# The lower steps of a tree of column maxima as one strided reduction, in a graph attention kernel

## What is computed

```
h = x @ W
e = leaky_relu((h @ a_src)[src] + (h @ a_dst)[dst], 0.2)
m = segment_max(e, dst)
ex = exp(e - m[dst])
out = segment_sum(ex * h[src], dst) / (segment_sum(ex, dst) + 1e-16) + b
```

## Time and profile before

| What | Value |
|---|---|
| Median of 3 runs | 9346.27 us (9345.22 to 9348.08) |
| The profiled execution | 9340.91 us |
| Its span, first to last instruction | 9339.1 us |
| Instructions | 124921 |
| VectorE busy | 7033.1 us (75%) |
| GpSimd busy | 6762.4 us (72%) |
| TensorE busy | 4710.7 us (50%) |
| ScalarE busy | 4614.9 us (49%) |

### The profile page before, as it was taken

One profiled execution on the slowest core, in us unless ns is written; L12 is line 12 of the kernel. 1 busy time (PEld: TensorE's weight loads), 2 busy tenths in 40 slices (PEclk: granted clock), 3 DMA queues, 4 the chain that ended last, 5 costly groups with the idle time before them and its releaser, 6 DMA issues. The chain is left out here.

```text
span 9339.1 us, 124921 instructions
## 1 busy us (share of the span) xinstructions
PE 4710.7 (50%) x23458; PEld 4311.8 (46%) x23458; DVE 7033.1 (75%) x11854; ACT 4614.9 (49%) x12210; POOL 6762.4 (72%) x6887
## 2 busy tenths in 40 slices
PE   5777777777344444444444444444443444444444
PEld 4666666666344444444443444444443333333333
DVE  6888888888557777777777777777776777777777
ACT  4777777777334444444443444444443444444443
POOL 4777777777237777777767777777776777777776
PEclk8666666666655555555555555555555555555555
DMA  2222222222111111111111111111111111111111
GB/s 70 55 55 55 57 55 55 55 55 55 54 44 31 31 31 31 31 31 31 31 27 30 31 31 31 31 31 31 31 31 28 33 32 32 33 32 32 33 33 29
DMA packets 674668, 358.57 MB, mean 38 GB/s; under 512 B 548403, under 2 KB 549299, under 8 KB 674243
## 3 DMA queue, kind: packets, MB, share of 16 engines
q0 software_dynamic: 219264, 236.37, 13.5%
q1 hardware_dynamic: 455354, 121.70, 6.4%
HBM read 334.11 MB, written 23.35 MB: 38 GB/s over the span
## 5 line engine op out<-in xcount | busy, mean ns | idle before, releaser
L1504 POOL DMA_INDIRECT plain_rows_in<-table,plain_idx x5139 | 4965.6, 966 | 1591.0 <-issue 1591.0
L1752 PE MATMUL plain_ps_sums<-plain_rows_in,plain_prob 128*125 x10908 | 2434.5, 412 | 7.7 <-ACT plain_prob L1715 7.7
L1752 PEld LDWEIGHTS plain_ps_sums<-plain_rows_in,plain_prob 128*125 128x125 f32 x10908 | 2374.6, 329 | 32.5 <-ACT plain_prob L1715 8.3
L970 POOL DMA_INDIRECT heads_rows_in<-h_in,heads_idx x1713 | 1781.6, 1040 | 529.1 <-issue 528.8
L1715 ACT ACTIVATE plain_prob<-plain_prob 128x2250 f32<-128x2250 f32 x300 | 623.6, 2079 | 1844.4 <-DVE plain_prob L1640 1844.4
L1773 PE MATMUL plain_ps_max<-ident,plain_column_max 128*125 128x128 f32 x300 | 172.9, 576 | 2527.2 <-DVE plain_column_max L1621 2527.2
L1773 PEld LDWEIGHTS plain_ps_max<-ident,plain_column_max 128*125 128x125 f32 x300 | 85.0, 283 | 2603.7 <-DVE plain_column_max L1621 2603.7
L1706 ACT ACTIVATE plain_score_sb<-plain_mask,plain_rows_in 128x125 f32<-128x125 f32 x1800 | 553.8, 386 | 1319.9 <-DMA plain_rows_in<-table,plain_idx 1319.9
L1615 DVE TENSOR_TENSOR plain_top<-plain_score_sb,plain_ps_score 128x750 f32<-128x750 f32 x300 | 280.7, 936 | 1148.7 <-ACT plain_ps_score L1706 1148.7
L1706 ACT ACTIVATE plain_ps_score<-plain_mask,plain_rows_in 128x125 f32<-128x125 f32 x3600 | 1058.9, 347 | 0.0
L1200 ACT ACTIVATE heads_masked<-heads_mask,heads_scores_sum 128x125 f32<-128x125 bf16 x3600 | 1052.2, 386 | 0.6 <-DVE heads_scores_sum L1035 0.2
(11 more groups left out here) (258 smaller groups left out, 7481.6 us busy)
## 6 DMA issues: line engine op xcount, KB each, us to landing
plain_rows_in<-table,plain_idx POOLq DMA_INDIRECT x5139, 2.4
heads_edges<-in_edge_attr SPq DMA_DIRECT2D x104, 544.0 KB
heads_rows_in<-h_in,heads_idx POOLq DMA_INDIRECT x1713, 2.4
plain_own<-table SPq DMA_DIRECT2D x312, 32.7 KB
table<-plain_out_sb SPq DMA_DIRECT2D x200, 32.7 KB
plain_unit_int<-unit_ints SPq DMA_DIRECT2D x312, 0.0 KB
plain_idx<-in_src SPq DMA_DIRECT2D x312, 8.5 KB
plain_idx<-in_src SPq DMA_DIRECT2D x312, 0.5 KB
```

Source lines behind the costliest of these rows:

```text
L970: gp.indirect_dma_start(rows_in[h][:, t, :], None, table[:, :], bass.IndirectOffsetOnAxis(ap=idx[h][:, t:t + 1], axis=0)).then_inc(done, 16)
L1504: gp.indirect_dma_start(rows_in[h][:, t, :], None, table[:, :], bass.IndirectOffsetOnAxis(ap=idx[h][:, t:t + 1], axis=0)).then_inc(done, 16)
L1752: ins = te.matmul(sums[h % 2], prob[h % 2][:, t, :], rows, start=t == 0, stop=t == Q - 1)
```

## The change

In weigh, three instructions of VectorE (maximum of three tiles with three, of one with one, of one with one, each with a wait for the one before) become one tensor_reduce. It reads top as 125 nodes of six elements each, which lie 125 elements (500 bytes) apart, and writes the same column_max with the same signal. STEPS, the number of steps of the chain's semaphore in a unit, falls from 19 to 17, as two waits go. Maxima are exact in any order, so the results stay the same.

```diff
--- before.py
+++ after.py
@@ -1528,7 +1528,7 @@
             @block.vector
             def _(ve):
                 rounds = unit_rounds(ve)
-                STEPS = 19
+                STEPS = 17
 
                 ve.wait_ge(w_loaded, 4 * 16 if next_weights else 16)
                 if next_weights:
@@ -1616,9 +1616,7 @@
                     ve.tensor_tensor(top[:, :, :], top[:, :, :], score_ps[:, THIRD:2 * THIRD, :], ALU.max
                                      ).then_inc(tops_made, 1)
                     ve.wait_ge(tops_made, n + 1)
-                    step(ve.tensor_tensor(top[:, 0:3, :], top[:, 0:3, :], top[:, 3:6, :], ALU.max))
-                    step(ve.tensor_tensor(top[:, 0, :], top[:, 0, :], top[:, 1, :], ALU.max))
-                    ve.tensor_tensor(column_max[:, :], top[:, 0, :], top[:, 2, :], ALU.max
+                    ve.tensor_reduce(column_max[:, :], top[:, :, :].rearrange("p t n -> p n t"), AX.X, ALU.max
                                      ).then_inc(columns_maxed, 1)
                     tile = prob[h % 2]
                     step(ve.scalar_tensor_tensor(tile[:, 0:THIRD, :], score_sb[:, :, :], SLOPE, score_sb[:, :, :],
```

## The result

The changed kernel takes 9390.7 us (9390.3 to 9396.3, 5 runs), the kernel before 9346.0 us (9343.6 to 9348.1, 5 runs): ratio 1.0049, 95% interval 1.0035 to 1.0064. It is slower by 45 us. I had forecast slower by 109 us, with a range from 9388; the sign holds, and so does what holds a gather; the size is 2.4 times too large, because of when a gather is held.

What follows compares the result with a forecast made beforehand. GpSimd's back-to-back gathers were taken as the bound. Longer holds by L1624 (+120 us) less escaping units (-11 us) gave +109 us on 9340.9, so 9450, against the median 9455; stated forecast 9454 us, range 9388 to 9475.

Steps and rivals of the forecast that it cites:

- what holds a gather: A VectorE instruction with two SBUF inputs holds a GpSimd gather until its end; the gather then needs 0.82 us more.
- The bound: Plain layers: GpSimd goes from gather to gather without waiting for data, so every nanosecond of hold is in the end time.
- need: The moment 0.12 us after a gather's start when it needs what a two-SBUF-input VectorE instruction has until its end.
- That a strided reduction holds nothing: Beside the new reduction in weigh, gather A was to take its unheld 0.94 us.
- D: Duration of the new 128x750 strided reduction, forecast 1.60 us, bounded between 0.94 and 1.87 us.
- my own formula: While L1624 catches B, each unit's end moves by D - 1.20: +0.40 us a unit, x 300 = +120 us.
- B: The gather after A in a plain-layer unit; forecast to need at 1.74 us and be held 0.74 us by L1624.
- the escape of units: Units where B needs before L1624 begins, so nothing is held: 11 of them at D = 1.60, -11 us.
- A: First held gather of a plain-layer unit (at 6010.75); needs 0.49 us after L1616's end, between 0.23 and 0.59 across units.
- The rival with the other sign: Reduction so long that L1624 begins after B's need, so today's holds vanish: -113 us, 9233 us; chance 0.09.
- turning point: D of 1.78 us, where half the units have escaped and the change in time is near zero.

Runs made afterwards that it cites:

- e1: Changed kernel with the scalar-tensor-tensor's second input taken from PSUM instead of SBUF: 9228.8 us, the kernel before 9365.9 us.
- e8: The changed kernel unaltered, on a second chip: 9326.4 us, the kernel before there 9365.5 us, ratio 0.9957.
- e16: The kernel before, unchanged, profiled on a third chip: 9365.0 us.
- e17: Changed kernel with one more wait, VectorE waiting for its own reduction before the scalar-tensor-tensor: 9232.3 us, the kernel before 9365.9 us.
- e2: Changed kernel plus an unused short reduction between its reduction and the scalar-tensor-tensor: 9234.0 us, the kernel before 9365.9 us.
- e5: Kernel before, three tree steps kept, with the maximum of the twelve tiles moved before the scalar-tensor-tensor: 9287.8 us, the kernel before 9365.5 us.
- e4: Changed kernel with the maximum that finishes the other twelve tiles moved before the scalar-tensor-tensor: 9234.8 us, the kernel before 9365.9 us.
- e6: Kernel before plus an unused short reduction between its three tree steps and the scalar-tensor-tensor: 9457.2 us, the kernel before 9365.5 us.
- e18: Changed kernel with the twelve-tile maximum before the scalar-tensor-tensor, and head_max as one strided reduction without L1052: 9296.9 us, the kernel before 9365.9 us.
- e9: The kernel before, unchanged, on a chip where every kernel took about 12 ms: 12279 us.

## Why the prediction was off

The steps, one by one.

The bound (GpSimd's train of gathers, each hold in full in the end time) was right for the plain layers. Over the twelve profiles of before, after, e1 to e8, e16 and e17 the span less the gathers' total is nearly a constant: 9339.1 - 4965.6 = 4373.5 before, 4376.1 after, and between 4374.9 (e1) and 4384.2 (e17) in the others, while the spans reach from 9224.0 to 9452.4.

What holds a gather (two SBUF inputs; 0.82 us more after the end) was right, and e1 shows it apart from length: 975 ns at most with one of the two inputs taken from PSUM. The trace of the kernel before shows it by count. Take the gathers whose need, 0.12 us after their start, lies at least 0.15 us behind the start of an instruction and 0.02 us before its end. All of them are held in L1619 (291), L1624 (297) and L1052 (198), and end 0.81 to 0.83 us after the instruction. None is held in L1616 (145, 949 ns at most) and L1627 (297, 961 ns at most), which have one input in PSUM, and none in the reduction L1053 (198, 949 ns at most). No need falls into L1620 or L1621, so that these two hold a gather is not shown. Of instructions that read one tensor and a scalar per partition from SBUF, L1068 holds none of 99 (947 ns at most), but of 94 gathers in L1610 of e2, 14 take 957 to 977 ns and end 0.81 to 0.82 us after it; such a hold is 33 ns at most.

That a strided reduction holds nothing was right: no first gather beside it is held (297 in the profile after, 954 ns at most).

D was off by little: 1.555 for 1.60. With D = 1.555 my own formula gives 300 x (1.555 - 1.20) = +106 us, so this is not the step that failed.

The step that failed is the one in which the scalar-tensor-tensor "runs from D - 0.06 to D + 0.88" and B "falls into it", with the escape of units whose A needs "before D - 1.31". I let it take what they share from its very start. It does so about 0.15 us later, so units escape where A needs before D - 1.16 = 0.40 us, not 0.25. In the first comparison that is 73 units and not a few. An escaped B would have been held for 2.44 - 1.25 - 0.34 = 0.85 us, with 0.34 the mean need of A among them; 73 x 0.85 = 62 us, and 106 - 62 = +44 us. Measured: +47 in the gathers' total, +45 in the medians.

The plain layers of the kernel before show nothing of this: there L1619 lets nearly all A go at once, 0.58 after L1616, and B's need, at 1.83, lies well inside L1624 (from 1.15). But the heads layer of the same trace shows it, and the prediction makes no use of that. L1038 has two SBUF inputs, and gathers happen to start just behind it:

```profile
1073.15 1.35 DVE L1038 TENSOR_TENSOR heads_edges<-heads_edges,heads_rows_in 128x1152 f32<-128x1152 f32 x1
1073.19 2.13 POOL L970 DMA_INDIRECT heads_rows_in<-h_in,heads_idx  x1 [0.30 <-issue]
...
1118.26 1.41 DVE L1038 TENSOR_TENSOR heads_edges<-heads_edges,heads_rows_in 128x1152 f32<-128x1152 f32 x1
1118.28 0.94 POOL L970 DMA_INDIRECT heads_rows_in<-h_in,heads_idx  x1 [0.30 <-issue]
```

The gather that starts 41 ns after L1038 is held to 0.82 us after its end; the one that starts 18 ns after it is free, and L1038 takes 1.41 us for the usual 1.35. A window that opens at the start would have held both. So the border between 18 and 41 ns could have been read before the forecast.

The rival with the other sign was priced right (-113 us; e2 -132 and e17 -134 on chips where the kernel before has 137 us of holds, 4986.5 less the 4849.1 of e1, and not 113) but placed wrongly: I put its turning point at D = 1.78. With the window at 0.15 it is, for the needs in the first comparison, at about 1.61, where nearly half the units escape, 0.05 us from D. (That is almost the D that I had forecast: the right window with my own D would have said hardly any change.) So the change sits on a steep slope, and a chain that is later by 0.08 us against the train is enough to turn +45 into -39 us. That the outcome depends on the chip was in none of my cases; the range of A's need between the units of one profile, 0.23 to 0.59, could have warned me. So the sign was partly luck, as it turns with the chip, and so was it that the time lies within my range: its lower end stood for a D of 1.75, and D was 1.555.

Where the two meet, the loser waits, on either side: a gather of 1.67 us behind L1622, and an L1622 of 1.00 us behind a gather. But the start that the profile shows does not decide who is first, as a scalar-tensor-tensor that started up to 27 ns earlier still lost; and a gather that came first held L1622 by 67 ns at most in the profile after, not for its whole 0.94 us. A tensor_tensor with both inputs in SBUF holds as the scalar-tensor-tensor does: the gather beside L1052 takes 1.66 us, and 53 us go with L1619's holds (e5 against e4).

## What to carry to other kernels

In a kernel in which GpSimd issues back to back and nothing else is full, as here, look at the spread of its instructions' durations, not at their mean. Here nearly every nanosecond above the median was in the end time (the span less the gathers' total stayed between 4373.5 and 4384.2 us, while the spans went from 9224.0 to 9452.4), and the ends of the long ones named the VectorE instruction that held them, by 0.82 us each. The VectorE instruction with two SBUF inputs then cost by where it stood against that train, not by its length: the same scalar-tensor-tensor of 128x750 goes with +92 us in e6 and with -134 us in e17. That was so where VectorE had time to spare (3.6 us a unit in the profile after; in e18 it seems to have had none). Behind the reduction, another order of two instructions, one more wait or a useless 0.27 us gave 1.4% over the kernel before. The version to keep is the reduction together with the order of e4 (9234.8 us against 9365.9). Each of these was run on one chip with the later phase; that e4 gains on a chip like that of the first comparison too is an estimate: in its profile the gather ahead of the scalar-tensor-tensor has its need at least 0.12 us before the start in every unit, which leaves 0.27 us to the window, while the phases of the chips differ by 0.08. A result that rests on such a phase must be measured on more than one chip.

## What the runs showed of the hardware that I had not expected

- A scalar-tensor-tensor with two SBUF inputs takes what it shares with an indirect DMA's issue on GpSimd about 0.15 us after its start in the profile, the DMA's issue 0.12 us after its own (estimates from starts and durations): of 297 second gathers in the profile after, all 224 held ones start at least 28 ns after the instruction and all 73 free ones earlier; on another chip 133 are held, from 27 ns on. The gather itself can hold the instruction, by up to 67 ns in the profile after (997 for 930).
- A reduction of 128x750 takes 0.935 us over adjacent elements and 1.555 at a stride of 500 bytes; at the same stride 1125 columns take 2.25 and 2250 columns 4.36 us: 0.17 us and 1.85 to 1.86 ns a column, for six, nine and eighteen tiles alike.
- The same kernel differs by 20 us between chips, and the holds account for it: they are 21 us longer in sum where gathers land 0.06 us later. That the landing is the cause is argued: ScalarE's times are the same, and no run varied the landing by itself.
- On two chips all kernels took about 12 ms; in the profile of e9 VectorE is idle up to 28.7 us at a time for what the profile calls remote. The cause stayed open.
